# Statistics, normalising, turning and router logits spread from a front stage into the first units of a transformer layer kernel

## The chip, the cores and the metric

The kernel runs on one core of one Trainium2 chip. The metric is the device time of one execution in microseconds (us), the median of several runs. The engines are TensorE (PE), VectorE (DVE), ScalarE (ACT), GpSimd (POOL) and SyncE (SP), which issues nearly all transfers. Each engine works through its own list in order and waits on semaphores for the others.

## The reference

```python
x = L0_attn_x                         # (16, 512, 256), float32
xn = layernorm(x)                     # no scale or shift, eps 1e-5
x = x + attention(xn) + ffn(xn)
# attention: 16 heads of 64, causal, out @ Wo + bo
# ffn: xn + shared_mlp(xn) + sum over the top 2 of 16 experts,
#      chosen by sigmoid(xn @ gate_w + gate_b), weights normalised to 1
# each mlp: (silu(x @ wg) * (x @ wu)) @ wd, hidden size 128
```

## The kernel before

There are B = 16 batches of T = 512 tokens, of width D = 256. A batch in SBUF is 128 partitions by QT = 4 slices by 256 (0.52 MB). Most products run in three passes on a high and a low part of each operand (`HI`, `LO`; `PASSES`), in a rounded 32-bit format; a low part is the value minus its high part.

**Front stage (`stage_a`).** For each batch: load x, `bn_stats` and `bn_aggr` on VectorE (`moments`), a square root on ScalarE, a reciprocal and four normalising operations on VectorE, a store of the normal rows to DRAM (`xn_rows`), eight transposes on TensorE (L280), two copies on ScalarE, and eight matmuls in full float32 for the router's logits (L290, token-major, 16 columns wide). Between these the attention weights, Wo and the shared expert's weights are loaded and split, the high parts on ScalarE and the low parts on GpSimd (L186). A sigmoid over all logits ends the stage; then all engines meet at a barrier.

**Stream (`stream`).** A unit is one pair of heads of one batch: UNITS = 128, eight per batch. `STEPS` goes from -3 to 131; step u works on different units at once: it turns and weighs the probabilities of unit u, makes the scores of u + 1, projects k, v and q for u + 2, and adds the output projection of u - 2. Steps -3 to -1 are the ramp. PSUM is a ring of 8 banks; `order(u)` lists which kinds of work take banks in a step and `emptied` gives the semaphore that frees each. A few times per step SyncE goes through `slot` 0 to 3, paced by TensorE (`pace`), and issues what belongs there.

Batch b's turned rows `xnt[b % 2]` are made in the stream once more, one batch ahead, in units 3, 11, 19, ...: SyncE reloads the normal rows (`load_normal`), TensorE turns them (`turn`, L758), ScalarE copies the high part (L890) and VectorE makes the low part (L1039). GpSimd adds x, the normal rows and bo (`prepare`, L1266 and L1268) in four steps of a batch.

The router's choice (`route`, VectorE, operations of 128x1024) runs in units 0 to 12; rows are scattered to their experts' queues in units 12 to 43 (`FIRST_SCATTER`), the expert tiles (`TICKS`, two per unit) run in units 49 to 89, and their results are gathered and added after that. SyncE clears the queues in DRAM in units 0 to 9 (L521).

Lines that the rows name: L663 projects k or q (six matmuls of 512 columns), L715 weighs v with the probabilities, L878 is ScalarE's copy of a unit's attention output, once per unit, L986 adds the mask and takes the maximum, L860 is the exponential, L1314 GpSimd's division of the probabilities, L979 VectorE's copy of turned probabilities.

## Time and profile before

| | |
|---|---|
| median of 3 runs | 1960.73 us (1960.04 to 1964.51) |
| profiled execution | 1962.58 us, its span 1960.9 us |
| TensorE busy | 1892.3 us (97% of the span) |
| VectorE, ScalarE, GpSimd busy | 72%, 62%, 52% |
| front stage, to the stream's first transfer | 97.2 us |

The span runs from the first to the last instruction. In the stream TensorE is almost always busy, in the front stage and the ramp it is not. The profile's rows give start and length in us; a group's mean is in ns.

### The profile page before, as it was taken

Reading aid. Unit: us, or ns where it says so; the run is one execution under the profiler, and the core shown is the slowest. Engines: PE = TensorE matmul, PEld = TensorE weight load, DVE = VectorE, ACT = ScalarE, POOL = GpSimd, SP = SyncE. Lnnn points to the kernel's source line nnn. Section 1 sums busy time; section 2 is a strip of 40 time slices with the busy share of each in tenths; the row PEclk is TensorE's granted clock in tenths of the full one; section 3 lists DMA queues with packets and bytes.
Section 4 is the critical chain, followed back from the end, with each engine's and each line's share of the span. In section 5 each row is a group of like instructions: output and inputs, shape, how many; then the busy total and the mean of one; then the engine's idle time right before and its main releaser. Section 6 shows DMA issues by size and latency. Waiting matters only on the chain.

```text
span 1960.9 us, 53515 instructions
## 1 busy us (share of the span) xinstructions
PE 1892.3 (97%) x20556; PEld 1748.2 (89%) x20558; DVE 1406.0 (72%) x4086; ACT 1218.2 (62%) x3340; POOL 1020.2 (52%) x1512
## 2 busy tenths in 40 slices
PE   5879999999999999999999999999999999999998
PEld 5868898888889898999999999999999999888897
DVE  7658886767676676666766667667667888878875
ACT  3355566666666565666665666666666666656564
POOL 2133447777776644344343343344344867687742
PEclk9999999999999999999999999999999999999999
DMA  8534422434343312544545445545432232333200
GB/s 246 192 109 175 153 94 82 138 106 146 109 146 109 114 68 71 194 153 148 175 157 178 147 154 167 171 162 173 147 103 77 87 119 87 114 95 120 70 29 12
DMA packets 158603, 249.92 MB, mean 127 GB/s; under 512 B 27280, under 2 KB 112528, under 8 KB 158352
## 3 DMA queue, kind: packets, MB, share of 16 engines
...
q14 instruction: 84, 0.69, 0.1%
...
## 4 chain that ended last, share of the span: by engine, by line
PE 65%; POOL 16%; issue 8%; DVE 3%; ACT 3%; DMA 0%; POOLq 0%; SPq 0%; DVEq 0%
PE d_bank L663 13%; PE d_bank L715 10%; POOL d_probs L1314 9%; PE d_bank L701 9%; PE d_bank L690 8%; PE d_bank L731 6%; PE d_bank L676 6%; PE d_bank L789 6%; POOL queued_rows L1277 4%; PE d_bank L776 3%; ACT d_probs L860 2%; PE d_bank L747 2%; DVE d_probs L986 1%; POOL d_rows L1305 1%; PE d_bank L799 1%
## 5 line engine op out<-in xcount | busy, mean ns | idle before, releaser
L1314 POOL TENSOR_SCALAR d_probs<-d_probs,d_inverse 128x512 f32<-128x512 f32 (+3 forms) x1024 | 554.7, 556 | 756.6 <-DVE d_inverse L992 755.3
L860 ACT ACTIVATE d_probs<-d_probs,d_bias 128x512 f32<-128x512 f32 (+3 forms) x1024 | 562.4, 553 | 119.4 <-DVE d_bias L986 119.4
L986 DVE CUSTOM_DVE_ANT_0 d_probs<-d_bank,mask 128x512 f32<-128x512 f32 (+3 forms) x1024 | 432.5, 484 | 3.2 <-PE d_bank L701 2.5
L663 PE MATMUL d_bank<-d_xnt,wqk_all 128*128 128x512 f32 x1536 | 414.0, 405 | 1.5 <-DVE d_xnt L1039 1.5
L663 PEld LDWEIGHTS d_bank<-d_xnt,wqk_all 128*128 128x128 f32 x1536 | 274.6, 191 | 54.9 <-DVE d_xnt L1039 1.7
L715 PE MATMUL d_bank<-d_probs_t,d_v 128*64 128x128 f32 x5120 | 308.9, 276 | 0.0
L701 PE MATMUL d_bank<-d_ks,d_qs 64*128 64x512 f32 (+3 forms) x3072 | 290.5, 332 | 8.3 <-issue 6.9
L715 PEld LDWEIGHTS d_bank<-d_probs_t,d_v 128*64 128x64 f32 x5120 | 278.1, 137 | 17.1 <-issue 5.4
L701 PEld LDWEIGHTS d_bank<-d_ks,d_qs 64*128 64x128 f32 x3072 | 251.8, 191 | 24.3 <-issue 7.7
L690 PEld LDWEIGHTS d_bank<-ident_r,d_probs_moved 64*128 64x128 f32 x5120 | 226.1, 136 | 48.5 <-issue 48.2
L690 PE MATMUL d_bank<-ident_r,d_probs_moved 64*128 64x64 f32 x5120 | 244.1, 245 | 22.8 <-POOL d_probs L1314 22.0
L853 ACT ACTIVATE d_probs_t<-d_bank 128x512 f32<-128x512 f32 (+1 forms) x384 | 188.2, 525 | 102.1 <-PE d_bank L690 91.9
L997 DVE TENSOR_TENSOR d_qs<-d_bank,d_qs 128x512 fp32r<-128x512 f32 x128 | 88.5, 691 | 201.6 <-ACT d_qs L866 201.6
L878 ACT ACTIVATE d_out_t<-d_bank 128x512 fp32r<-128x512 f32 x128 | 76.4, 597 | 249.5 <-PE d_bank L715 249.5
L979 DVE COPY d_probs_t<-d_bank 128x512 f32<-128x512 f32 (+1 forms) x384 | 209.1, 591 | 8.4 <-PE d_bank L690 7.9
L731 PEld LDWEIGHTS d_bank<-wo_all,d_out_t 128*128 128x128 f32 x1536 | 201.1, 190 | 12.2 <-issue 1.7
L676 PEld LDWEIGHTS d_bank<-wv_all,d_xnt 128*128 128x128 f32 x1536 | 199.4, 190 | 11.1
L731 PE MATMUL d_bank<-wo_all,d_out_t 128*128 128x256 f32 x1536 | 206.7, 281 | 1.5 <-DVE d_out_t L1008 1.5
L676 PE MATMUL d_bank<-wv_all,d_xnt 128*128 128x256 f32 x1536 | 201.2, 281 | 0.0
L860 ACT ACTIVATION_READ_ACCUMULATOR d_probs<-d_probs,d_bias 128x1 f32 x1024 | 194.8, 190 | 0.0
L1008 DVE TENSOR_TENSOR d_out_t<-d_bank,d_out_t 128x512 fp32r<-128x512 f32 x128 | 88.2, 689 | 111.6 <-ACT d_out_t L878 110.7
L1305 POOL DMA_INDIRECT d_rows<-routed_rows,slot x128 | 132.1, 1032 | 34.6 <-issue 34.6
(122 smaller groups left out, 2292.6 us busy)
## 6 DMA issues: line engine op xcount, KB each, us to landing
queued_rows<-d_zeros SPq DMA_DIRECT2D x79, 256.0 KB, 2.4
d_x<-queued_rows SPq DMA_DIRECT2D x79, 256.0 KB, 3.4
routed_rows<-d_y SPq DMA_DIRECT2D x79, 256.0 KB, 2.3
...
a_x_in<-in_L_attn_x SPq DMA_DIRECT2D x16, 512.0 KB, 7.5
xn_rows<-a_xn SPq DMA_DIRECT2D x16, 512.0 KB, 5.2
d_normal<-xn_rows SPq DMA_DIRECT2D x32, 256.0 KB, 3.7
d_base<-in_L_attn_x SPq DMA_DIRECT2D x32, 256.0 KB, 2.9
```

The lines of the kernel that those rows point to most:

```text
L663: last = pe.matmul(to[:, :], wqk[:, n % PAIRS, "qk".index(kind), wa, k, :], xnt[n // PAIRS % 2][:, xb, k, :], start=first, stop=(k == KD - ...
L676: last = pe.matmul(to[:, t * 2 * P:(t + 1) * 2 * P], xnt[b % 2][:, xa, k, tok * P:(tok + 1) * P], wv[:, wb, k, cols], start=(k == 0 and (x ...
L690: last = pe.transpose(to[r][:, off:off + DK].bitcast(F32R), moved[half(r), i, h, j * P:(j + 1) * P], ident[half(r), half(r)])
L701: last = pe.matmul(to[h][:, at * P:at * P + cols], qs[r][qa][half(h), i * P:(i + 1) * P], ks[r][kb][half(h), 0:cols], start=(n == 0), stop ...
L715: last = pe.matmul(to[half(h), i * P:(i + 1) * P], v[u // 2 % 2][:, j, col:col + DK], probs_t[fill][:, h, at + j, :], start=(j == 0), stop ...
L731: last = pe.matmul(to[:, s * D:(s + 1) * D], out_t[g % 2][oa][:, j, cols], wo[:, wb, g % 4 * GROUP + j, :], start=(j == 0 and n == 0), sto ...
L853: act.activation(probs_t[fill][:, :, :, half(0)], bank(f"t{fill}", u)[:, 0:2 * slots * DK].rearrange("p (h j n) -> p h j n", h=2, n=DK), A ...
L860: act.activation(part, part, ACT.Exp, bias=bias[:, i, h:h + 1], scale=-1.0, accum_out=total[which][:, at % 4:at % 4 + 1]).then_inc(exp_don ...
L979: dve.tensor_copy(probs_t[fill][:, :, :, half(1)], bank(f"t{fill}", u, 1)[:, 0:2 * slots * DK].rearrange("p (h j n) -> p h j n", h=2, n=DK ...
L986: dve.tensor_tensor_reduce(out=probs[:, i, h, 0:cols], in0=bank(f"s{fill}", u, h)[:, at * P:at * P + cols], in1=mask[:, T - cols:T], scale ...
L1305: pool.indirect_dma_start(out=rows[m % 4 // 2][:, m % 2 * 2 + n, :], out_offset=None, in_=dram["routed"][:, :], in_offset=bass.IndirectOff ...
L1314: pool.tensor_scalar(part, part, inverse[which][:, at % 4:at % 4 + 1], 1.0, ALU.mult, ALU.mult).then_inc(norm_done, 1)
```

## The change

The front stage keeps the loads and splits of the weights, the gate's weights among them (now in high and low parts), and the statistics of the first four batches (`KEPT`), which stay in SBUF as `xa`; it normalises batch 0. Low parts are shared between VectorE (`ON_DVE`) and GpSimd (`ON_POOL`), and the scale of q's weights goes into the one copy.

In the stream the other twelve batches' rows are loaded for their statistics alone (`load_ahead`) through three buffers, four batches at the end of each of the steps -3, -2 and -1, with one square root for four batches (`deviation`). `FRONT` gives the places where batch n is taken in, two per step, from (-3, second part) for batch 0 to unit 5 for batch 15: GpSimd normalises its rows one place ahead (`normalise_rows`), SyncE stores them, TensorE turns them (`turn`), ScalarE and VectorE make the high and low parts, and one place later six matmuls of 512 columns and 16 output rows make the logits expert-major (`logits`), which ScalarE copies and TensorE turns back one place later still (`logits_back`). The turned rows go to DRAM in high and low parts (`xnt_split`, 1.05 MB per batch) and are loaded for use one batch ahead (`load_xnt`, units 6, 14, ...); the turns of units 3, 11, ... are gone. The rows of batches 4 to 15 are loaded a second time into `xa` (`load_xa`). The sigmoid runs in unit 6. Routing, clearing, scatter and expert tiles all move by `ROUTE_AT` = 7 units.

```diff
 FLEX_AT = 229344 - 32 * 1024
-FIRST_SCATTER = 12
+ROUTE_AT = 7
+FIRST_SCATTER = ROUTE_AT + 12
+KEPT = 4
+GROUPS = [range(b, b + 4) for b in range(KEPT, B, 4)]
...
+                for n, (src, view, _) in enumerate(loads):
+                    sp.dma_start(view, src).then_inc(stage_loaded[n], DMA)
+                    if n < KEPT:
+                        sp.dma_start(xa[n][:, :, :], x_src[n]).then_inc(x_loaded[n], DMA)
+                for n, name in enumerate(("wg", "wu", "wd")):
+                    src = ins["L0_ffn_shared_" + name]
+                    to = shared_in[:, n * WPART:(n + 1) * WPART]
+                    if n < 2:
+                        to, src = to.rearrange("p (k f) -> p k f", k=KD), src.rearrange("(k p) f -> p k f", p=P)
+                    sp.dma_start(to, src).then_inc(stage_loaded[len(loads)], DMA)
 
             @block.gpsimd
             def _(pool):
...
+                pool.tensor_tensor(gate_w[:, LO, :, :], gate_in[:, :, :], gate_w[:, HI, :, :].bitcast(F32), ALU.subtract
+                                   ).then_inc(gate_split, 1)
+                for n in ON_POOL:
+                    _, view, parts = loads[n]
                     pool.wait_ge(stage_hi, n + 1)
                     pool.tensor_tensor(parts[LO], staged_like(view, parts[HI]), parts[HI].bitcast(F32), ALU.subtract
...
-                    if n < KD:
-                        act.activation(view, view, ACT.Copy, scale=-SCALE).then_inc(scaled, 1)
...
+                act.wait_ge(const_loaded, 2 * DMA)
+                act.activation(gate_w[:, HI, :, :], gate_in[:, :, :], ACT.Copy).then_inc(gate_hi, 1)
+                for n in range(len(loads)):
+                    split(n)
+                act.wait_ge(stage_loaded[len(loads)], 3 * DMA)
...
             @block.vector
...
+                def split(n):
+                    _, view, parts = loads[n]
+                    dve.wait_ge(stage_hi, n + 1)
+                    dve.scalar_tensor_tensor(parts[LO], staged_like(view, parts[HI]), -SCALE if n < KD else 1.0,
+                                             parts[HI].bitcast(F32), ALU.mult, ALU.subtract).then_inc(split_dve, 1)
+
+                for b in range(KEPT):
+                    moments(b)
+                    gather(b)
+                    if b < KD:
+                        split(ON_DVE[b])
+                dve.wait_ge(std_done, 1)
+                dve.reciprocal(rstd[:, 0:KEPT * QT], rstd[:, 0:KEPT * QT]).then_inc(rstd_done, 1)
+                dve.wait_ge(rstd_done, 1)
+                for q in range(QT):
+                    dve.tensor_scalar(xa[0][:, q, :], xa[0][:, q, :], mean_var[:, q, 0:1], rstd[:, q:q + 1],
+                                      ALU.subtract, ALU.mult).then_inc(first_normal, 1)
+                split(ON_DVE[KD])
 
...
+        ahead_x = [base[1][:, :, :].rearrange("p q d -> p (q d)"),
+                   *(nc.alloc_sbuf_tensor_at(f"d_ahead_x{hl}", [P, GROUP * T], F32, offset=out_at + (HALVES + hl) * GROUP * T * 4)[:, :]
+                     for hl in range(HALVES))]
...
+        FRONT = {place: n for n, place in enumerate([(-3, 1)] + [(u, part) for u in range(-2, B // 2 - 2) for part in range(2)] + [(B // 2 - 2, 0)])}
...
+                def load_xa(b):
+                    sp.wait_ge(*xn_kept(b - KEPT))
+                    sp.wait_ge(n_ready, (b - KEPT + 1) * KD)
+                    for part in range(2):
+                        two = slice(part * 2, part * 2 + 2)
...
+
+                def store_turned(b, hl):
+                    sp.wait_ge(n_out, (b + 1) * KD)
+                    for k in range(KD):
+                        sp.dma_start(turned_rows(b, hl, k), turned(b)[:, hl, k, :].bitcast(F32)).then_inc(ax_stored[b % 2], DMA)
+
...
+                def load_xnt(b, hl, k):
+                    if hl == 0 and k == 0:
+                        sp.wait_ge(ax_stored[b % 2], (b + 1) // 2 * KD * HALVES * DMA)
+                        if b == 1:
+                            sp.wait_ge(ax_stored[0], (B // 2 - 1) * KD * HALVES * DMA)
+                            sp.wait_ge(lg_ready, B - 1)
+                        else:
+                            sp.wait_ge(p_ready, 2 * PAIRS * (b - 1))
+                            sp.wait_ge(v_ready, PAIRS * (b - 1))
+                    sp.dma_start(xnt[b % 2][:, hl, k, :].bitcast(F32), turned_rows(b, hl, k)).then_inc(xnt_loaded[b % 2], DMA)
+
+                LATER = {place: KEPT + len(ahead_x) + n for n, place in enumerate(
+                    [(-3, slot) for slot in range(4)] + [(-2, 3)] + [(-1, slot) for slot in range(4)])}
+
+                def load_ahead(b):
+                    n = b - KEPT
+                    if n >= len(ahead_x):
+                        sp.wait_ge(stats_done, n - len(ahead_x) + 1)
+                    sp.dma_start(ahead_x[n % len(ahead_x)].rearrange("p (q d) -> p q d", q=QT), x_src[b]
+                                 ).then_inc(ahead_loaded[n % len(ahead_x)], DMA)
 
                 def clear(n):
+                    if n == 0:
...
 
-                        for n in range(u * 8 + slot * 2, u * 8 + slot * 2 + 2):
+                        n = FRONT.get((u, slot // 2))
+                        if n is not None and n <= B:
+                            if slot % 2 == 0 and n < B:
+                                store_xn(n)
+                            if n >= 2:
...
+                def turn(n):
+                    if n:
+                        pe.wait_ge(x_normal, n * QT)
                     for k in range(KD):
-                        to = take(f"n{k}", u)
+                        to = take(f"n{k}", n)
                         for q in range(QT):
-                            last = pe.transpose(to[:, q * P:(q + 1) * P].bitcast(F32R), normal[:, q, k * P:(k + 1) * P],
+                            last = pe.transpose(to[:, q * P:(q + 1) * P].bitcast(F32R), xa_r[n % KEPT][:, q, k * P:(k + 1) * P],
                                                 ident[:, :])
                         last.then_inc(n_ready, 1)
+
+                def logits(n):
+                    to = take("lg", n)
+                    pe.wait_ge(n_out, (n + 1) * KD)
+                    first = True
+                    for k in range(KD):
+                        for wa, xb in PASSES:
+                            last = pe.matmul(to[0:E, :], gate_w[:, wa, k, :], turned(n)[:, xb, k, :], start=first,
+                                             stop=(k == KD - 1 and (wa, xb) == PASSES[-1]))
+                            first = False
+                    last.then_inc(lg_ready, 1)
+
+                def logits_back(n):
+                    to = take("lb", n)
+                    pe.wait_ge(al_done, n + 1)
+                    for q in range(QT):
+                        last = pe.transpose(to[:, q * P:q * P + E].bitcast(F32R), al[:, q * P:(q + 1) * P], ident[0:E, 0:E])
+                    last.then_inc(lb_ready, 1)
 
                 def count(kind, u):
 
@@ -801,6 +831,13 @@
                     last.then_inc(xt_ready, 1)
...
                     act.wait_ge(hidden_done, u // PAIRS + 1)
@@ -932,6 +984,7 @@
                         exponential(3, 1, u + 1)
                         exponential(1, 0, u + 1)
                         exponential(1, 1, u + 1)
+                    front_part(u, 0)
...
-                        split_normal(u)
+                    front_part(u, 1)
+                    if u < 0:
+                        deviation(u + len(GROUPS))
+                    if u == B // 2 - 2:
+                        act.wait_ge(lg_out, B)
+                        act.activation(gates[:, :, :], gates[:, :, :], ACT.Sigmoid).then_inc(sig_done, 1)
...
+                    last.then_inc(mean_done, 1)
+
+                def deviation(g):
+                    cols = slice(GROUPS[g][0] * QT, (GROUPS[g][-1] + 1) * QT)
+                    dve.wait_ge(std_done, g + 1)
+                    dve.reciprocal(rstd[:, cols], rstd[:, cols]).then_inc(rstd_done, 1)
 
                 steps = [0]
...
+                    if u < 0:
+                        for b in GROUPS[u + len(GROUPS)]:
+                            moments(b)
...
+                def normalise_rows(n):
+                    if n >= KEPT:
+                        pool.wait_ge(xa_loaded[n % KEPT], n // KEPT * 2 * DMA)
+                        pool.wait_ge(rstd_done, (n - KEPT) // 4 + 1)
+                    for q in range(QT):
+                        col = n * QT + q
+                        pool.tensor_scalar(xa[n % KEPT][:, q, :], xa[n % KEPT][:, q, :], keep["mean_var"][:, col, 0:1],
+                                           keep["rstd"][:, col:col + 1], ALU.subtract, ALU.mult).then_inc(x_normal, 1)
+
+                normalise_rows(1)
...
```

## Rows read from the trace of the kernel before

**Rows 1.** The page, part 1: busy time of each engine.

```profile
PE 1892.3 (97%) x20556; PEld 1748.2 (89%) x20558; DVE 1406.0 (72%) x4086; ACT 1218.2 (62%) x3340; POOL 1020.2 (52%) x1512
```

**Rows 2.** Windows: length, busy per engine, PEclk, DMA share, GB/s.

```profile
0.00:10.00 10.00, 0.00 (x0) 0.00 (x0) 3.40 (x15) 3.17 (x4) 1.42 (x9) 1.00 0.65 210
...
0.00:27.00 27.00, 13.32 (x75) 13.17 (x75) 16.80 (x71) 11.76 (x20) 3.78 (x10) 1.00 0.81 228
```

**Rows 3.** Groups by form, first 97 us.

```profile
L186 POOL TENSOR_TENSOR wo_all<-a_staged,wo_all 128x2048 fp32r<-128x2048 f32 x1 | 4.5, 4546 | 4.0 <-ACT wo_all L212 4.0
```

**Rows 4.** Timeline of the front stage: start, length, engine, line.

```profile
0.80 0.43 SPq L145 DMA_DIRECT2D a_x_in<-in_L_attn_x  x1
...
4.81 1.41 DVE L236 BATCH_NORM_STATS2 a_stats<-a_x_in 128x6 f32<-128x256 f32 x4 [4.81 <-DMA a_x_in<-in_L_attn_x]
...
6.25 0.38 DVE L240 BATCH_NORM_AGGREGATE a_mean_var<-a_stats 128x2 f32<-128x6 f32 x4
...
10.26 1.38 DVE L251 TENSOR_SCALAR a_xn<-a_x_in,a_mean_var,a_rstd 128x256 f32<-128x256 f32 x4
...
27.14 3.42 DVE L251 TENSOR_SCALAR a_xn<-a_x_in,a_mean_var,a_rstd 128x256 f32<-128x256 f32 x4
...
27.76 2.34 POOL L186 TENSOR_TENSOR wqk_all<-a_staged,wqk_all 128x1024 fp32r<-128x1024 f32 x1 [2.06 <-ACT wqk_all L212]
```

**Rows 5.** Timeline of the seam and the ramp.

```profile
97.23 0.80 SPq L517 DMA_DIRECT2D d_normal<-xn_rows  x2
...
110.69 1.28 ACT L860 ACT_TABLE_LOAD   x1
...
112.46 0.69 DVE L986 CUSTOM_DVE_ANT_0 d_probs<-d_bank,mask 128x512 f32<-128x512 f32 x1 [1.07 <-PE d_bank L701]
...
116.03 2.27 POOL L1314 TENSOR_SCALAR d_probs<-d_probs,d_inverse 128x512 f32<-128x512 f32 x4 [11.20 <-DVE d_inverse L992]
...
119.36 0.99 DVE L979 COPY d_probs_t<-d_bank 128x512 f32<-128x512 f32 x2
```

**Rows 6.** Timeline, ScalarE: the starts of L878 in chosen units.

```profile
134.09 0.60 ACT L878 ACTIVATE d_out_t<-d_bank 128x512 fp32r<-128x512 f32 x1 [1.58 <-PE d_bank L715]
...
203.92 0.60 ACT L878 ACTIVATE d_out_t<-d_bank 128x512 fp32r<-128x512 f32 x1 [4.03 <-PE d_bank L715]
...
243.36 0.60 ACT L878 ACTIVATE d_out_t<-d_bank 128x512 fp32r<-128x512 f32 x1 [3.03 <-PE d_bank L715]
...
344.71 0.60 ACT L878 ACTIVATE d_out_t<-d_bank 128x512 fp32r<-128x512 f32 x1 [2.57 <-PE d_bank L715]
...
371.80 0.60 ACT L878 ACTIVATE d_out_t<-d_bank 128x512 fp32r<-128x512 f32 x1 [2.57 <-PE d_bank L715]
...
384.30 0.60 ACT L878 ACTIVATE d_out_t<-d_bank 128x512 fp32r<-128x512 f32 x1 [1.59 <-PE d_bank L715]
...
409.55 0.60 ACT L878 ACTIVATE d_out_t<-d_bank 128x512 fp32r<-128x512 f32 x1 [3.10 <-PE d_bank L715]
...
1870.87 0.60 ACT L878 ACTIVATE d_out_t<-d_bank 128x512 fp32r<-128x512 f32 x1 [2.58 <-PE d_bank L715]
...
1885.40 0.60 ACT L878 ACTIVATE d_out_t<-d_bank 128x512 fp32r<-128x512 f32 x1 [0.99 <-PE d_bank L715]
...
1897.18 0.60 ACT L878 ACTIVATE d_out_t<-d_bank 128x512 fp32r<-128x512 f32 x1 [2.38 <-PE d_bank L715]
...
1908.96 0.60 ACT L878 ACTIVATE d_out_t<-d_bank 128x512 fp32r<-128x512 f32 x1 [2.85 <-PE d_bank L715]
```

**Rows 7.** Transfers issued in the first 100 us; last: KB, us to landing.

```profile
a_x_in<-in_L_attn_x SPq DMA_DIRECT2D x16, 512.0 KB, 7.5
...
d_normal<-xn_rows SPq DMA_DIRECT2D x2, 256.0 KB, 3.0
```

**Rows 8.** Groups by form on GpSimd, 400 to 420 us.

```profile
L1314 POOL TENSOR_SCALAR d_probs<-d_probs,d_inverse 128x256 f32<-128x256 f32 x4 | 1.9, 478 | 0.0
...
L1266 POOL TENSOR_TENSOR d_base<-d_base,d_normal 128x256 f32<-128x256 f32 x1 | 0.7, 749 | 0.0
```

352 lines of the change are left out of this document (175 added, 177 removed).

## Prediction

> **What bounds the kernel now.** I read the page's busy times first: TensorE is busy 97% of the span and no other engine over 72% [rows 1]. So in the long stream a microsecond taken from or given to TensorE counts whole, and one on VectorE, ScalarE or GpSimd counts only where TensorE ends up waiting. Next the timeline at the seam of the two stages: SyncE issues the stream's first transfer at 97.23 us, the first probabilities are copied at 119.36 us, and unit 0's attention output is ready at 134.09 us, where TensorE has taken over as the bound [rows 5, 6]. The change works in these first 134 us and in the first units. Last, the starts of L878, which runs once per unit, right after TensorE finishes a unit's weighing; their distances are the units' lengths [rows 6].
>
> I call the barrier between stages t0. Before, unit 0 is done at t0+36.9 (134.09 less 97.23) and the first copy of probabilities comes at t0+22.1.
>
> **The front stage.** It loses sixteen batches of turning, fp32 logits, normalising and storing; what is left is bound by loads. It loads six weight halves of 0.52 MB, Wo with 1.05, four batches of 0.52 and 0.39 of shared weights: 6.7 MB. In the first 27 us the trace moves 228 GB/s at a share of 0.81, so 281 GB/s when the engines are full; 6.7 MB take 23.8 us. The first load lands 4.0 us after its issue at 0.80, some 2.4 us more than its own transfer, so the last lands near 27 us [rows 2, 4]. Behind it on GpSimd: ScalarE's high part of Wo ends at about 28.0, GpSimd's low part takes 4.55 [rows 3], to 32.5, and the shared low part about 1.9 more, to 34.4. On VectorE: the square roots come after ScalarE's last copy and a table load, about 30.5, then the first batch's normalising and one low part (the nearest row is four slices of normalising in 1.38 [rows 4]; for 128x1024 I take 1.2, an estimate from that rate). Alone this would end at 33.3. But four such slices took 3.42 instead of 1.38 while GpSimd ran a low part [rows 4], so I let VectorE get through only when GpSimd's Wo is done, at 32.5: 35.7, and 36 with the barrier. Bounds: 34.7 if nothing collides, 43 if loads run at 210 GB/s, the rate of the first 10 us [rows 2]. The term: 36.0 - 97.2 = **-61.2**.
>
> The Trainium skill ("SBUF — State Buffer", section SBUF: two separate sides) says that VectorE and GpSimd share a port pair which one takes for a whole instruction. By that rule, the trace agrees with it here, 3.42 against 1.38; it would lock the two engines against each other in the stage's last 6 us, and not in the later units, where VectorE reads PSUM with one SBUF operand. Without it the stage would be 1.3 us shorter.
>
> **The ramp (steps -3 to -1).** Twelve batches' statistics now stand in VectorE's order, four at the end of each step, each 1.41 + 0.38 = 1.8 us [rows 4]. VectorE, in order, counted from t0:
> Loads 4 to 6 are issued at once, the first lands after 4.0 [rows 4]. Batch 7 waits for a free buffer (about 5.5), then lands by 10. Four moments end at 12.0.
> Step -2 can't end before batch 2 is turned. Its rows are normalised by GpSimd, behind `prepare(0, 0)`, and that waits for the reload of batch 0's normal rows, which SyncE issues only behind `load_ahead(10)`, at 12.5. With 8.7 us of transfers queued in that stretch (8, 9, 10, two stores, this load) it lands near 18. Then two operations of 0.75, four slices of 0.48 [rows 8]: 21.4. Turning (1.3), copies and differences: 24.5. This is the wait that takes the place of the front stage's: VectorE's moments of 8 to 11 and `load_ahead(11)` are queued behind it.
> Moments 8 to 11: 24.5 to 32.1.
> Step -1: root and reciprocal 0.6; a table switch back to the exponential, 1.28 [rows 5]; the maxima, exponentials and normalising for unit 0. Before, GpSimd had done its first four at 118.3, 5.8 us after the first maximum's start at 112.46 [rows 5]. So 39.8; `prepare` 1.5; rows of batch 4, 1.9; turning 1.3; copies and differences 1.9: 46.4.
> Moments 12 to 15 last 7.2 if the data are there. `load_ahead(14)` stands on SyncE behind the store of batch 4 (43.2), and `load_ahead(15)` waits for batch 12's statistics, at 47.8 and then some 5 to 5.5 of landing with stores ahead of it, so the last moments end near 54.9; root and reciprocal: 55.5. Only now does VectorE copy unit 0's probabilities, 33.4 later after t0 than before. From that copy to unit 0's output were 14.7 [rows 5, 6]; one more table switch adds 1.3, the front's work on TensorE is run ahead meanwhile. Unit 0 is done at t0+71.5: **+34.6**. Bounds: +24, if each load lands as fast as the 3.0 of a lone reload, no collision, and GpSimd is never late; +48, if each of the four loads named lands after the 7.5 that loads took in the busy front stage [rows 7].
> The Trainium skill ("ScalarE: Activation LUTs", section What ACT_TABLE_LOAD costs) gives 2.66 us for a switch, with a drain, where the row has 1.28 [rows 5] and shows no drain; the five switches of the ramp and unit 6 would cost 7 us more if all lay on the path. I go by the row.
>
> **Units 1 to 5** each take in two batches. TensorE per batch: eight turns, 0.72 (unit 19, with them, 12.50; unit 123, without, 11.78); six logits matmuls of 512 columns, 0.229 each (unit 121 with twelve such takes 14.53, unit 122 11.78): 1.37; four narrow turns back, at the price of a turn, 0.36. That is 2.45, or 4.9 a unit [rows 6]. The steady units of the same kinds, 17 to 21, took 64.84; less one turn, plus 24.5: 88.6. Before, units 1 to 5 took 203.92 - 134.09 = 69.83 [rows 6]. The term: **+18.8**. It holds as long as TensorE stays the bound. VectorE adds 3.2 a unit and ScalarE 3.6, less than TensorE; GpSimd adds eight slices, 3.8 [rows 8], in gaps where it waits for VectorE's inverses.
> **Unit 6**: four narrow turns and, on ScalarE, the sigmoid with two table loads, 0 to 3.6 on the path. I take 2.0: **+2.4**.
>
> **Routing moved by seven units.** It runs VectorE's long steps of 128x1024. Before, units 1 to 8 took 109.27, units 9 to 16, of the same kinds, 101.35 [rows 6]: 7.9 too much, of which 5.0 in units 1 to 5 are gone from the term above already and 2.9 in units 6 to 8. I let the 7.9 come back in units 7 to 15, where the 2.9 leave: **+5.0** (bounds -3 and 8). Scatter, expert tiles and gathers move as they are and end at unit 125 of 128, still under TensorE: 0.
>
> **Turns taken out of the later stream**: fourteen (units 11, 19, ... 115) at 0.72 [rows 6]: **-10.1**. In their place are transfers: per batch 1 MB stored and 1 MB loaded, the loads a whole batch ahead, hidden in the steady units. For batch 1 alone the load waits for the last store, with about 11 us of TensorE's work to cover 5 to 7: 0, else up to 4.
>
> The sum: -61.2 + 34.6 + 18.8 + 2.4 + 5.0 - 10.1 = -10.5. The profiled execution took 1962.58; 1952.1. The median of the runs is 1.85 below it: **1950.2, told as 1951**.
>
> **The rivals.**
> *The ramp is starved.* Each of the four loads that VectorE waits for lands 3 us later, as in the front stage (7.5 [rows 7]): +13, so 1964. For it: about 15 MB move in 55 us of ramp, 270 GB/s. Against it: the rate of 281.
> *Transfers set the pace of units 0 to 5.* Each unit loads, stores and stores turned two batches: 4.2 MB, with base and normal rows 4.3. In my 17.4 us that is 247 GB/s; TensorE would wait for rows to turn. At 210 GB/s [rows 2] a unit takes 20.5, and six of them +18: 1969, slower than before. It decides from 1.8 us per unit on (224 GB/s), where the gain is gone. Against it: these are 1 to 2 KB runs at 281 GB/s or better.
> *The ramp and routing cost less.* The moments overlap, and moved routing finds slack in its new place: -5 and -8: 1938.
> *The front stage doesn't shrink as far*: within the bounds of 34.7 and 43 above, at worst +7; it is a part of the range, not a case.
>
> **How the numbers follow.** Forecast 0.48, starved ramp 0.20, transfers 0.16, cheap ramp 0.16. The forecast's own range is 1942 to 1960. The likeliest gives 1951; cutting 0.1 at each end of the cases gives 1932 to 1974. A measurement of this kernel tells about 0.3% (5.9 us) from no change, so "faster" is under 1954.9. The forecast case lies there with 0.37 of its 0.48 (0.10 same, 0.01 slower), the cheap ramp whole; the starved ramp is 0.02 faster, 0.10 same, 0.08 slower; transfers 0.03 same, 0.13 slower. Faster 0.55, same 0.23, slower 0.22.
>
> **What the profile after should show.** The stream's first transfer at 35 to 38 us, with GpSimd or VectorE last. The moments in three blocks, VectorE waiting for loads in the first and last, and for GpSimd's rows in the second. The first copy of probabilities at 91, unit 0's L878 at 107.5. L878 spaced by 16.5 to 19.5 in units 1 to 5. Unit 11 and its likes 0.7 shorter. I am wrong if units 1 to 5 are over 19 each, if TensorE waits there for GpSimd's rows, if unit 0 comes before t0+60 or after t0+85, or if narrow logits matmuls cost other than 0.23.

## The result and the profile after

The changed kernel is slower, by 0.7%: 1973.75 us median (1971.92 to 1974.03, 4 runs), the kernel before beside it 1960.38 (1957.36 to 1964.51, 4 runs), a ratio of 1.007, 95% interval 1.005 to 1.009. Its profiled execution took 1973.66 us, the span 1971.9.

The page, part 1, answers [rows 1]. TensorE does 22.6 us less work and the span is 11 us longer, so it stands idle longer:

```profile
PE 1869.7 (95%) x20334; PEld 1704.5 (86%) x20334; DVE 1381.9 (70%) x4017; ACT 1209.2 (61%) x3314; POOL 1089.1 (55%) x1570
```

**The end of the front stage**, timeline. The stage ends at 38.26 where it ended at 97.23 [rows 5]:

```profile
27.77 1.91 ACT L168 ACTIVATE wo_all<-a_staged 128x2048 fp32r<-128x2048 f32 x1 [2.02 <-DMA a_staged<-in_L_attn_Wo]
...
29.76 4.50 POOL L157 TENSOR_TENSOR wo_all<-a_staged,wo_all 128x2048 fp32r<-128x2048 f32 x1 [3.93 <-ACT wo_all L168]
...
32.35 4.50 DVE L211 TENSOR_SCALAR xa<-xa,mean_var,rstd 128x256 f32<-128x256 f32 x4
34.21 1.85 POOL L160 TENSOR_TENSOR shared_all<-a_shared_in,shared_all 128x768 fp32r<-128x768 f32 x1
36.77 1.21 DVE L199 SCALAR_TENSOR_TENSOR wv_all<-a_staged,wv_all 128x1024 fp32r<-128x1024 f32 x1
38.26 0.37 SPq L503 DMA_DIRECT2D d_base<-in_L_attn_x  x1
```

ScalarE waits for Wo until 27.8, where the forecast had the last load near 27. Behind it VectorE's four slices of normalising take 4.50 us where they take 1.38 alone [rows 4]. They start beside GpSimd's low part of Wo and get through only as GpSimd's operations finish: the first slice takes 2.05 us and ends 0.15 behind the low part of Wo, the second 1.89 and ends 0.15 behind the shared one, the other two 0.40 each; GpSimd's two take 4.50 and 1.85, no more than in the kernel before (4.5 [rows 3], and 1.85 in its L189). The Trainium skill ("SBUF — State Buffer", section SBUF: two separate sides) calls the port pair of VectorE and GpSimd an exclusive lock and no split of bandwidth; these rows agree.

**The ramp and the first units.** Timeline of chosen lines:

```profile
57.81 0.72 POOL L1358 TENSOR_TENSOR d_base<-d_base,d_normal 128x256 f32<-128x256 f32 x1 [13.49 <-DMA d_normal<-xn_rows]
...
59.32 9.66 POOL L1415 TENSOR_SCALAR xa<-xa,mean_var,rstd 128x256 f32<-128x256 f32 x8
...
64.21 1.25 PE L770 MATMUL d_bank<-ident_r,d_xa_r 128*128 128x128 f32 x8 [7.75 <-POOL xa L1415]
...
66.83 1.40 DVE L1116 BATCH_NORM_STATS2 stats<-d_ahead_x 128x6 f32<-128x256 f32 x4
...
75.06 1.08 DVE L1116 BATCH_NORM_STATS2 stats<-d_ahead_x 128x6 f32<-128x256 f32 x3 [3.00 <-DMA d_ahead_x<-in_L_attn_x]
...
97.20 1.40 DVE L1116 BATCH_NORM_STATS2 stats<-d_ahead_x 128x6 f32<-128x256 f32 x4 [1.25 <-DMA d_ahead_x<-in_L_attn_x]
...
101.55 1.41 DVE L1116 BATCH_NORM_STATS2 stats<-d_ahead_x 128x6 f32<-128x256 f32 x4 [2.54 <-DMA d_ahead_x<-in_L_attn_x]
...
103.92 1.55 DVE L1036 COPY d_probs_t<-d_bank 128x512 f32<-128x512 f32 x3
```

The eight slices of two batches' rows, 2 and 3, take 9.66 us on GpSimd, 1.2 each and not 0.48. TensorE waits 7.75 for the first four of them, VectorE's next statistics (66.83) stand behind the turning, and the first copy of probabilities (103.92) behind three blocks of statistics. Groups by form on GpSimd, 38 to 130 us, of the changed kernel:

```profile
L1415 POOL TENSOR_SCALAR xa<-xa,mean_var,rstd 128x256 f32<-128x256 f32 x28 | 33.9, 1220 | 2.3 <-POOLq L123 2.3
...
L1406 POOL TENSOR_SCALAR d_probs<-d_probs,d_inverse 128x256 f32<-128x256 f32 x6 | 2.8, 483 | 0.0
```

Both rows are `tensor_scalar` with two steps on the same shape. L1406, as L1314 before it [rows 8], multiplies by one operand per partition and by the constant 1; L1415 takes two operands per partition, subtracts the mean and multiplies by the inverse of the deviation, and costs 2.5 times as much.

**The units.** ScalarE's copy of a unit's output is L913 now and answers to L878 [rows 6]: units 0, 5, 16, 120, 121, 122, 123 and the last.

```profile
121.04 0.60 ACT L913 ACTIVATE d_out_t<-d_bank 128x512 fp32r<-128x512 f32 x1 [1.61 <-PE d_bank L728]
...
207.43 0.60 ACT L913 ACTIVATE d_out_t<-d_bank 128x512 fp32r<-128x512 f32 x1 [1.76 <-PE d_bank L728]
...
353.05 0.60 ACT L913 ACTIVATE d_out_t<-d_bank 128x512 fp32r<-128x512 f32 x1 [2.43 <-PE d_bank L728]
...
1873.85 0.60 ACT L913 ACTIVATE d_out_t<-d_bank 128x512 fp32r<-128x512 f32 x1 [3.05 <-PE d_bank L728]
1891.16 0.60 ACT L913 ACTIVATE d_out_t<-d_bank 128x512 fp32r<-128x512 f32 x1 [0.99 <-PE d_bank L728]
1904.31 0.60 ACT L913 ACTIVATE d_out_t<-d_bank 128x512 fp32r<-128x512 f32 x1 [2.34 <-PE d_bank L728]
1918.74 0.60 ACT L913 ACTIVATE d_out_t<-d_bank 128x512 fp32r<-128x512 f32 x1 [3.17 <-PE d_bank L728]
...
1962.77 0.60 ACT L913 ACTIVATE d_out_t<-d_bank 128x512 fp32r<-128x512 f32 x1 [5.91 <-PE d_bank L728]
```

Against [rows 6]: unit 0 comes 13.1 us earlier, unit 5 is 3.5 late, unit 16 8.3, unit 120 only 3.0, the last one 10.6 (1962.77 against 1952.15 before). The forecast had unit 0 26.6 us earlier. So there are three places of loss: up to unit 0; in the units from 17 to 120, which give back 5.4 and not 9.4; and behind unit 120, where nothing was put down.

Windows of the changed kernel: the ramp with unit 0, the units from 1 on, and unit 121 (length, busy per engine, PEclk, DMA share, GB/s):

```profile
38.26:121.04 82.78, 52.52 (x316) 37.90 (x316) 44.17 (x164) 29.60 (x69) 43.99 (x55) 0.71 0.66 222
121.00:220.00 99.00, 99.00 (x1038) 83.65 (x1038) 62.63 (x184) 65.08 (x168) 70.12 (x88) 1.00 0.70 231
...
1873.85:1891.16 17.31, 16.43 (x156) 14.49 (x156) 12.86 (x34) 8.96 (x24) 14.44 (x21) 0.90 0.37 108
```

In units 1 to 5 TensorE is busy all the time: transfers don't set their pace. In unit 121 GpSimd is busy 14.44 of 17.31 us and VectorE 12.86; before, in the same unit (14.53 us long), they were busy 9.46 and 10.68, and TensorE all the time at a granted clock of 1.00. Now TensorE stands idle for 0.9 us and the clock is 0.90 over the unit: 0.50, the level of 1.2 GHz, from 1877 to 1879, partly so in the microsecond on either side, and 1.00 elsewhere. Lines of the timeline there:

```profile
1872.76 2.51 POOL L1406 TENSOR_SCALAR d_probs<-d_probs,d_inverse 128x384 f32<-128x384 f32 x4
...
1874.95 0.98 DVE L1276 SCALAR_TENSOR_TENSOR d_acc<-d_rows,weight,d_acc 128x256 f32<-128x256 f32 x2
1875.41 0.84 PE L703 MATMUL d_bank<-ident_r,d_probs_moved 64*128 64x64 f32 x16 [0.50 <-POOL d_probs L1406]
1875.43 1.09 POOL L1397 DMA_INDIRECT d_rows<-routed_rows,slot  x1 [0.16 <-issue]
...
1875.86 0.68 DVE L1065 TENSOR_TENSOR d_out_t<-d_bank,d_out_t 128x512 fp32r<-128x512 f32 x1
1876.63 3.55 PE L714 MATMUL d_bank<-d_ks,d_qs 64*128 64x512 f32 x24 [0.38 <-issue]
...
1882.05 1.00 POOL L1397 DMA_INDIRECT d_rows<-routed_rows,slot  x1 [0.31 <-issue]
...
1883.09 2.29 POOL L1406 TENSOR_SCALAR d_probs<-d_probs,d_inverse 128x512 f32<-128x512 f32 x4
...
1891.05 1.18 PE L703 MATMUL d_bank<-ident_r,d_probs_moved 64*128 64x64 f32 x24
```

GpSimd issues six gathers of 1.0 to 1.1 us, one every 1.3 us, between two groups of divisions. The group behind them ends at 1885.4 and TensorE turns its output at 1891.05 without a wait: that one isn't late. TensorE's two waits come earlier. The first, 0.50, is for the group ahead of the gathers, which takes 2.51 us where the next such group takes 1.85: VectorE adds gathered slices beside it (L1276). Its inverses were ready at 1871.6, and GpSimd, which came out of the six gathers of the unit before only at 1869.0 and had other divisions and two additions ahead of it, got to it at 1872.8. The second, 0.38, has no releaser in the profile, but ends 0.09 us after VectorE's L1065, which stands behind the same additions and gives back the bank of unit 120's output. TensorE's waits of 1.07 at 1893.98 and of 0.38 at 1906.91 end 0.10 us after L1065 too. With the slow clock, the scores of L714 then take 3.5 us to the next line where they took 2.05 in this unit before. From 1871 to 1925 there are 20 gathers, before there were 4, and for each a slice is added to the sums (22 of 0.58 us, before 4).

### The profile page after: what moved, and what is told of

Same layout as the page of the kernel before. It is cut to its first block, busy times and chain, and to the rows that moved or that the text cites. A ratio compares the mean times of both kernels' runs of the same rounds, so it can differ in the third digit from the quotient of the medians.

```text
span 1971.9 us, 53180 instructions
## 1 busy us (share of the span) xinstructions
PE 1869.7 (95%) x20334; PEld 1704.5 (86%) x20334; DVE 1381.9 (70%) x4017; ACT 1209.2 (61%) x3314; POOL 1089.1 (55%) x1570
## 4 chain that ended last, share of the span: by engine, by line
PE 64%; POOL 16%; issue 8%; DVE 4%; ACT 3%; DMA 2%; SPq 0%; POOLq 0%; DVEq 0%
PE d_bank L676 12%; PE d_bank L728 10%; POOL d_probs L1406 9%; PE d_bank L714 8%; PE d_bank L703 8%; PE d_bank L744 6%; PE d_bank L689 6%; PE d_bank L819 6%; POOL queued_rows L1369 4%; PE d_bank L806 3%; ACT d_probs L895 2%; PE d_bank L760 2%; DVE d_probs L1043 1%; POOL d_rows L1397 1%; PE d_bank L829 1%
## 5 line engine op out<-in xcount | busy, mean ns | idle before, releaser
L1406 POOL TENSOR_SCALAR d_probs<-d_probs,d_inverse 128x512 f32<-128x512 f32 (+3 forms) x1024 | 560.2, 561 | 739.1 <-DVE d_inverse L1049 737.9
L714 PE MATMUL d_bank<-d_ks,d_qs 64*128 64x512 f32 (+3 forms) x3072 | 293.5, 333 | 16.8 <-ACT d_probs_t L888 9.8
L714 PEld LDWEIGHTS d_bank<-d_ks,d_qs 64*128 64x128 f32 x3072 | 254.8, 192 | 32.3 <-ACT d_probs_t L888 10.5
L913 ACT ACTIVATE d_out_t<-d_bank 128x512 fp32r<-128x512 f32 x128 | 76.6, 599 | 255.3 <-PE d_bank L728 255.3
L1054 DVE TENSOR_TENSOR d_qs<-d_bank,d_qs 128x512 fp32r<-128x512 f32 x128 | 88.6, 692 | 199.4 <-ACT d_qs L901 198.1
L744 PEld LDWEIGHTS d_bank<-wo_all,d_out_t 128*128 128x128 f32 x1536 | 202.7, 189 | 12.7 <-issue 1.7
L1065 DVE TENSOR_TENSOR d_out_t<-d_bank,d_out_t 128x512 fp32r<-128x512 f32 x128 | 88.3, 690 | 119.5 <-ACT d_out_t L913 118.4
```

The source lines that it names most:

```text
L714: last = pe.matmul(to[h][:, at * P:at * P + cols], qs[r][qa][half(h), i * P:(i + 1) * P], ks[r][kb][half(h), 0:cols], start=(n == 0), stop ...
L744: last = pe.matmul(to[:, s * D:(s + 1) * D], out_t[g % 2][oa][:, j, cols], wo[:, wb, g % 4 * GROUP + j, :], start=(j == 0 and n == 0), sto ...
L1406: pool.tensor_scalar(part, part, inverse[which][:, at % 4:at % 4 + 1], 1.0, ALU.mult, ALU.mult).then_inc(norm_done, 1)
```

## The experiments

### The tail: expert tiles seven units later, alone

`tiles_late` is the kernel before with one edit, `before_again` the kernel before once more, in a single run.

```diff
-FIRST_TICK = FIRST_SCATTER + 2 * B + 5
+FIRST_TICK = FIRST_SCATTER + 2 * B + 5 + 7
```

> The kernel before with the expert tiles, and so the gathers behind them, seven units later, and nothing else: front stage, ramp, turns and routing stay. Theory (gathers cost at the end): results are then gathered and added in units 98 to 125 instead of 91 to 118, three items in units 118 to 121 instead of one, two in units 122 to 125 instead of none, where GpSimd and VectorE have no slack; the last units grow by 7 to 8 us in all and the kernel takes about 1968. Rival (the tail is long for another reason, as the transfers or lower clock of the changed kernel): within 2 us of the kernel before, 1959 to 1963.

> The kernel before, unchanged, for its trace on the chip that the next kernels run on. In the two traces so far the changed kernel's steady units are about 0.1 us longer than the same units of the kernel before (for instance 11.96 against 11.87), which eats the 0.7 us per batch that the removed turns should give back. If this is the chip, the units here are as long as in the changed kernel (11.95 or so for a plain unit of the steady stretch). If it is the changed kernel (its transfers of turned rows, or where its tiles lie), they stay at 11.87.

`tiles_late`: 1963.26 (10 runs), before 1959.88 (21 runs), ratio 1.0021 (1.0011 to 1.0030). Its copies of units 120 to 123, timeline:

```profile
1865.88 0.60 ACT L878 ACTIVATE d_out_t<-d_bank 128x512 fp32r<-128x512 f32 x1 [2.96 <-PE d_bank L715]
1883.13 0.60 ACT L878 ACTIVATE d_out_t<-d_bank 128x512 fp32r<-128x512 f32 x1 [0.99 <-PE d_bank L715]
1896.19 0.60 ACT L878 ACTIVATE d_out_t<-d_bank 128x512 fp32r<-128x512 f32 x1 [2.26 <-PE d_bank L715]
1910.70 0.60 ACT L878 ACTIVATE d_out_t<-d_bank 128x512 fp32r<-128x512 f32 x1 [3.16 <-PE d_bank L715]
```

The lengths are 17.25, 13.06 and 14.51, those of the changed kernel (17.31, 13.15, 14.43) and not 14.53, 11.78, 11.78 [rows 6]. From unit 120 to the last this kernel takes 87.1 us, `before_again` 81.4 (1872.4 to 1953.8). So moving the tiles lengthens the last units by itself, by 5.7, where 7 to 8 were expected. The median grew by only 3.4, under the expected 1968, and the traces show one reason: units 17 to 120, which the tiles leave and enter, take 1523.1 us against 1526.2 in the first trace of the kernel before and 1530.6 in `before_again`. The move gains something there.

`before_again` took 1964.21, with plain units of 11.86 to 11.87 as in the first profile, so the 0.1 us of the changed kernel's units isn't the chip's. The two traces of the unchanged kernel differ by 2.3 us in the front stage (97.2, 94.9), 1.2 in the ramp with unit 0 and 4.5 in units 17 to 120; terms taken from one trace each are known no better than that.

### The ramp: what GpSimd's rows cost

`one_pointer` is the changed kernel with GpSimd multiplying by the inverse deviation alone and an immediate in place of the second operand; the mean is left out of the rows of batches 1 to 15.

```diff
-pool.tensor_scalar(xa[n % KEPT][:, q, :], xa[n % KEPT][:, q, :], keep["mean_var"][:, col, 0:1],
-                   keep["rstd"][:, col:col + 1], ALU.subtract, ALU.mult).then_inc(x_normal, 1)
+pool.tensor_scalar(xa[n % KEPT][:, q, :], xa[n % KEPT][:, q, :], keep["rstd"][:, col:col + 1], 1.0,
+                   ALU.mult, ALU.mult).then_inc(x_normal, 1)
```

> The changed kernel, but GpSimd's normalising in the stream multiplies by the deviation's inverse and the constant 1 and no longer subtracts the mean (so the output leaves the mean out for batches 1 to 15): one operand per partition read from SBUF in place of two. Theory: the second such operand is what makes a slice of 128x256 take 1.23 us where the division of probabilities of the same size takes 0.48; a slice takes about 0.48, each batch's rows come 3 us sooner, and unit 0 is ready 7 to 9 us sooner after the front stage, so about 1965. Rival (GpSimd is slowed by VectorE beside it, or by the operand's place): slices stay near 1.2 us, and the time near 1974. A third: slices get short but SyncE's queue and the loads then hold VectorE, so under 4 us are won.

1965.17 (1963.35 to 1967.39, 10 runs), before 1959.88, ratio 1.0032 (1.0022 to 1.0042), 8.6 us under the changed kernel. Groups by form, as above:

```profile
L1415 POOL TENSOR_SCALAR xa<-xa,rstd 128x256 f32<-128x256 f32 x33 | 15.2, 485 | 2.3 <-POOLq L123 2.3
```

485 ns, the price of the divisions: the operand of the mean costs the other 0.74 us. The edit takes away two things together, the second operand per partition and the subtraction; no run has one without the other. Unit 0 comes at 114.7, 6.3 earlier, where 7 to 9 were expected.

### The ramp: statistics later

`late_moments` takes the statistics of batches 8 to 15 out of steps -2 and -1 and does them in steps -1, 0 and 1; their loads and roots move with them (left out of the cut).

```diff
+MOMENTS_AT = {-3: range(4, 8), -1: range(8, 11), 0: range(11, 14), 1: range(14, 16)}
...
-for b in GROUPS[u + len(GROUPS)]:
+for b in MOMENTS_AT.get(u, ()):
```

> The changed kernel with the statistics spread wider: batches 4 to 7 in step -3 as now, 8 to 10 in step -1, 11 to 13 in unit 0, 14 and 15 in unit 1, with the roots behind units 0 and 1. Theory: VectorE's blocks of statistics and their loads stand on the chain to unit 0 in steps -2 and -1 (from about 67 to 77 and from 92 to 103.4 us in the trace), while in units 0 and 1 TensorE is the bound and VectorE has room; unit 0 comes 12 to 18 us sooner, units 0 and 1 grow by up to 4, so 1960 to 1965. Rival: the chain is held by GpSimd's rows anyway, and unit 0 comes at most 5 us sooner (1969 or more).

1966.64 (6 runs), ratio 1.0041 (1.0028 to 1.0054). The copies of units 0 and 1:

```profile
105.29 0.58 ACT L915 ACTIVATE d_out_t<-d_bank 128x512 fp32r<-128x512 f32 x1
...
132.60 0.57 ACT L915 ACTIVATE d_out_t<-d_bank 128x512 fp32r<-128x512 f32 x1
```

Unit 0 is 15.7 us earlier, but the next unit takes 27.3 where it took 18.2, and at unit 16 only 4.4 are left. Most of the block's cost moved with it, and the time is above the 1960 to 1965 expected.

### Wo's low part, and the first batches' rows, on VectorE

`wo_on_dve` exchanges Wo for a weight half among the low parts and puts VectorE's last one ahead of its wait for the root:

```diff
-ON_DVE, ON_POOL = (0, 1, 5), (2, 3, 4, 6)
+ON_DVE, ON_POOL = (0, 1, 6), (2, 3, 4, 5)
...
+split(ON_DVE[KD])
 dve.wait_ge(std_done, 1)
...
-split(ON_DVE[KD])
```

> The changed kernel with the low part of Wo made by VectorE and that of v's second half by GpSimd, in the front stage alone. Theory: GpSimd's Wo (29.8 to 34.3 us) and VectorE's first batch that stood blocked behind it (4.50 instead of 1.38) set the end of the stage; now it ends at 34.5 to 36 instead of 38.3, and the whole is 2 to 4 us shorter, 1970 to 1972. Rival: loads or the root set the end, and the stage still ends at 38.

1970.01 (5 runs), before 1959.30 (24 runs), ratio 1.0050 (1.0034 to 1.0066): 3.7 under the changed kernel, as expected. The front stage ends at 35.1, unit 0 comes at 118.1.

`rows_and_wo_on_dve` adds that VectorE normalises batches 1 to 4, in the order in which it is free for them; GpSimd starts with batch 5.

```diff
+                normalise_rows(1)
                 for u in STEPS:
...
+                    if u == -1:
+                        normalise_rows(4)
                     front_part(u, 0)
...
+                    if u == -3:
+                        normalise_rows(2)
+                        normalise_rows(3)
...
-                    if n is not None and n + 1 < B:
+                    if n is not None and FIRST_ON_POOL <= n + 1 < B:
```

> The changed kernel with the rows of batches 1 to 4 normalised by VectorE (1 to 3 at the start of the stream, while it waits for loads, 4 in step -1; GpSimd does 5 to 15), and Wo's low part on VectorE as in the run beside it. Theory: GpSimd's 4.85 us per batch and its place behind the reload of normal rows leave the chain to unit 0: from the front stage's end to unit 0 in 65 to 71 us instead of 82.7, the front stage 3 shorter, 1957 to 1963 in all. Rival: loads hold VectorE's statistics, and only the 3 us that GpSimd's second batch cost are won: 1967 to 1970.

1955.67 (1952.21 to 1958.44, 10 runs), before 1959.30, ratio 0.9985 (0.9973 to 0.9997), less than the 1957 to 1963 expected. Timeline: VectorE's eight slices for batches 2 and 3, and the copy of unit 0:

```profile
37.77 2.66 DVE L1135 TENSOR_SCALAR xa<-xa,mean_var,rstd 128x256 f32<-128x256 f32 x8
```

```profile
104.99 0.60 ACT L914 ACTIVATE d_out_t<-d_bank 128x512 fp32r<-128x512 f32 x1 [1.44 <-PE d_bank L729]
```

VectorE takes 2.66 for what took GpSimd 9.66, both with two operands per partition. Unit 0 is at 105.0, that is t0+69.9, where the forecast had t0+71.5 for a ramp with cheap rows in another order; in `wo_on_dve`, without the move of the rows, it was t0+82.9. Units 1 to 5 are unchanged (18.25, 16.85, 16.85, 17.54, 16.92).

`rows_wo_spread` is this kernel with eight of the statistics in pairs in steps -1 to 2.

> As the run beside it, and the statistics spread two batches a step: 4 to 7 in step -3, then 8 and 9 in step -1, two each in units 0, 1 and 2, roots behind units 0 and 2. Theory: nothing but the first four batches' statistics is left ahead of unit 0, which comes 45 to 52 us after the front stage; units 0 to 2 pay 4 to 8 us of it back, since VectorE's lists there grow by 3.6 us each; 1945 to 1953, faster than both kernels. Rival: what unit 0 wins, units 0 and 1 give back wholly, as three quarters of it were in the run with late statistics, and the time is that of the run beside it.

1958.40 (10 runs), ratio 0.9992 (0.9980 to 1.0004). Unit 0 comes at 93.0, 12 us earlier, the next units take 20.9, 25.3 and 20.6, and unit 5 comes at 194.3, later than the 191.4 without it. The expected 1945 to 1953 was missed and the rival held: a pair of statistics in a unit, with its loads and roots, costs more there than in the ramp.

### The steady units: where the stream's tiles lie

A plain steady unit is 0.1 us longer in the changed kernel (units 33 to 34), in which the stream's tiles begin at byte 92800 of a partition and not at 92096, because 708 bytes were taken ahead of them to hold logits. `shifted_tiles` is the kernel before with an unused tile of that size there.

```diff
+sb("spare", [P, 177])                 # ahead of the stream's tiles
```

> The kernel before with an unused tile of 708 bytes per partition placed where the changed kernel has one, so that every tile of the stream lies 704 or 708 bytes further on, and nothing else. Repeated traces have a plain steady unit at 11.87 us in the kernel before and at 11.97 in the changed kernel and each variant of it. Theory (where the tiles lie): the units here are 11.97 too, and the kernel takes 8 to 11 us longer, 1968 to 1971. Rival (the transfers of turned rows, the semaphores waited for, or the order of PSUM banks): units stay at 11.87 and the time at 1960.

1966.42 (8 runs), before 1959.30, ratio 1.0031 (1.0018 to 1.0044). Copies of units 33 and 34 in the kernel before and in `shifted_tiles`:

```profile
563.65 0.60 ACT L878 ACTIVATE d_out_t<-d_bank 128x512 fp32r<-128x512 f32 x1 [0.99 <-PE d_bank L715]
575.51 0.60 ACT L878 ACTIVATE d_out_t<-d_bank 128x512 fp32r<-128x512 f32 x1 [2.57 <-PE d_bank L715]
```

```profile
563.40 0.60 ACT L878 ACTIVATE d_out_t<-d_bank 128x512 fp32r<-128x512 f32 x1 [0.99 <-PE d_bank L715]
575.37 0.60 ACT L878 ACTIVATE d_out_t<-d_bank 128x512 fp32r<-128x512 f32 x1 [2.67 <-PE d_bank L715]
```

11.86 and 11.97, and the changed kernel has 11.97 (571.91 to 583.88): an unused tile alone makes a plain steady unit 0.1 us longer. The time grew by 7.1, a little under the 8 to 11 expected. TensorE doesn't wait in either unit; its own matmuls take longer. From the projection of k to the start of the weighing, in the same two kernels:

```profile
567.34 1.65 PE L663 MATMUL d_bank<-d_xnt,wqk_all 128*128 128x512 f32 x6
...
573.06 2.40 PE L715 MATMUL d_bank<-d_probs_t,d_v 128*64 128x128 f32 x40
```

```profile
567.10 1.66 PE L663 MATMUL d_bank<-d_xnt,wqk_all 128*128 128x512 f32 x6
...
572.91 2.40 PE L715 MATMUL d_bank<-d_probs_t,d_v 128*64 128x128 f32 x40
```

5.72 against 5.81 us, 0.03 more in each of three kinds of matmul: the projections of k and q together, that of v, and the output projection. The weighing takes 2.33 from its start to the next line in both.

I then tried 772 bytes in place of 708, which puts the tiles at the same remainder by 256 as in the kernel before: in the kernel before, in the changed kernel, and in `rows_and_wo_on_dve`.

> The kernel before with the same unused tile of 772 bytes, so that its stream's tiles start at byte 92864. Theory: units at 11.86 to 11.87 and no change in time (1958 to 1961), where the tile of 708 bytes made them 11.97 and cost 7 us. Rival: 11.97 and 1965 or more.

> The changed kernel with its unused tile 64 bytes per partition longer: the stream's tiles start at byte 92864 instead of 92800; in the kernel before it is 92096. 92864 and 92096 leave the same rest by 128 and by 256, 92800 another. Theory (the start counts by its rest): plain steady units are back at 11.86 to 11.87, and the kernel takes 5 to 9 us less than the changed one, 1965 to 1969. Rival (where a tile lies counts in larger steps, or the distance to the tiles in front): units stay at 11.97 and the time at 1974.

> The version with the rows of batches 1 to 4 and Wo's low part on VectorE, and the tile 64 bytes longer. If the three causes add up (GpSimd's rows 14, the front stage 3, the tiles' place 7): 1947 to 1951, faster than the kernel before by 0.5%. If the place counts for nothing here: 1955.

1967.77 (5 runs), 1972.88 (5) and 1955.47 (11), before 1960.11 (20 runs); ratios 1.0036, 1.0066 and 0.9982, each as without the 64 bytes, units of 11.96 to 11.98. The theory, a rule of the remainder by 256 alone, fell. Four single runs of the kernel before with other shifts (64, 256, 512 and 832 bytes):

> The kernel before with an unused tile of 68 bytes, so that the stream's tiles start 64 bytes further on (92160 instead of 92096). A step at any other start: a plain steady unit takes 11.97 instead of 11.87. If only a long way counts: 11.87.

> The kernel before with the stream's tiles 256 bytes further on. If the start counts by its rest by 128 or 256: a plain steady unit at 11.87. If another start always costs: 11.97.

> The kernel before with the stream's tiles 512 bytes further on. If the start counts by its rest by 512: a plain steady unit at 11.87. If another start always costs: 11.97.

> The kernel before with the stream's tiles 832 bytes further on, the longest way that there is room for. If there is a threshold between 512 and 704 bytes: 11.97. If some starts are good and others not without such order: either.

| tiles begin at | plain units (33 to 34; 46 to 47) | time |
|---|---|---|
| 92096 (before) | 11.86; 11.78 | 1960.38 (1 run beside these) |
| +64, +832 | 12.01, 12.02; 11.93 | 1971.86, 1970.18 (1 run each) |
| +256, +512, +768 | 11.98, 11.97, 11.98; 11.89 | 1964.46, 1964.62 (1 run each), 1967.77 (5 runs) |
| +704 | 11.97; 11.91 | 1966.42 (8 runs) |

Starts with one remainder by 256 (64 and 832; 256, 512 and 768) do give one length, but the unshifted start has the remainder of the second row and is still the fastest. In these runs the distance to the tiles at fixed addresses changes as well, so either could be what counts; that stays open.

`after_tiles_back` puts the tiles of the changed kernel back at 92096. The logits' rows go, in two halves of 1 KB, where routing's tiles come later, ScalarE copies them in two steps, and one small tile of routing moves out of the way.

```diff
-sb("spare", [P, 177])
...
-keep["al_rows"] = nc.alloc_sbuf_tensor_at("al_rows", [E, T], F32, offset=al_at)
+al_at = [nc.sbuf_base - 4 * TT * 4 - SLOT_TILES * 4, FLEX_AT + 119 * 256]
+keep["al_rows"] = [nc.alloc_sbuf_tensor_at(f"al_rows{n}", [E, T // 2], F32, offset=at) for n, at in enumerate(al_at)]
```

> The changed kernel with the stream's tiles back at the address that they have in the kernel before (92096; the changed kernel has them at 92800). The 2 KB of the logits' rows, which needed the room in front of them, are split into two halves of 1 KB kept where routing's own tiles come later, so ScalarE copies them in two steps of 256 columns. Theory of placement: the plain steady unit falls from 11.97 back to 11.87, which over units 17 to 119 gives back 8 to 10 us, and a little more in the last units: 1962 to 1965 where the changed kernel has 1973.75. Rival: the 0.1 us of the changed kernel comes from its own work (rows turned loaded from DRAM in the steady units) and only looks like that of the placement: units stay at 11.97 and the time at 1972 to 1975. Second rival, from the looks in which every shift of the kernel before, 64 to 832 bytes, made units slower: it is the distance to the tiles of fixed address that counts; it gives the same as the theory here, as both come back together.

1964.68 (1960.39 to 1967.36, 12 runs), before 1960.40 (17 runs), ratio 1.0023 (1.0014 to 1.0032): 9.1 us under the changed kernel. Units 33 and 34:

```profile
570.79 0.60 ACT L914 ACTIVATE d_out_t<-d_bank 128x512 fp32r<-128x512 f32 x1 [0.99 <-PE d_bank L728]
582.66 0.60 ACT L914 ACTIVATE d_out_t<-d_bank 128x512 fp32r<-128x512 f32 x1 [1.84 <-PE d_bank L728]
```

11.87 again. The 0.1 us was the placement's and not that of the transfers which replaced the turns. It isn't in every unit: against the changed kernel, 54 of the 104 units from 17 to 120 are 0.04 to 0.2 us shorter, 4.9 us in all. The other 3.0 of the 7.9 us between the two traces come in jumps of single units, up to 2 us and both ways, such as also differ between the two traces of the unchanged kernel. The 9.1 in the medians is the firmer number.

### The best version

`last_four_late` is `rows_wo_64_on` with the statistics of batches 12 to 15 alone moved, two each to units 0 and 1. `last_four_tiles_back` is the same with the tiles back at 92096.

> As the run beside it, and only the last four batches' statistics moved, two behind unit 0 and two behind unit 1, with their rows (12 to 14) loaded ahead in step -1 so that VectorE needn't wait for them. Theory: the two earlier spreads gave their gain back because VectorE waited in units 0 and 1 for loads (1.6 us once) and because everything of three steps met there; with the loads ahead, 3 to 6 of the 7.4 us block in step -1 stay won: 1943 to 1947. Rival: VectorE's and ScalarE's lists in units 0 and 1 are full in any case (the root's two table loads, two batches taken in), and the time is that of the run beside it or 2 us more.

> The best version so far (rows of batches 1 to 4 normalised on VectorE, Wo's low part on VectorE, the last four batches' statistics in units 0 and 1; 1955.28) with the same tiles back at 92096. Theory of placement: the two gains add, 1944 to 1947, a ratio of 0.992 to 0.994 to the kernel before. Rival: the gain of placement was bought by the waits of the ramp or the tail and doesn't come: 1953 to 1957.

`last_four_late`: 1955.28 (1951.74 to 1957.34, 9 runs), ratio 0.9975 (0.9966 to 0.9985), which its parent's interval (0.9972 to 0.9992) overlaps; the expected 1943 to 1947 was missed and the rival held: unit 0 comes at 97.9 and not 105.1, unit 5 at 189.9 and not 191.5. `last_four_tiles_back`: 1948.20 (1943.80 to 1951.39, 6 runs), before 1960.40, ratio 0.9934 (0.9918 to 0.9949), the fastest of all and just above the 1944 to 1947 expected. Its profiled execution was the slowest of the six. The copies of units 0 and 5:

```profile
97.14 0.60 ACT L917 ACTIVATE d_out_t<-d_bank 128x512 fp32r<-128x512 f32 x1 [2.63 <-PE d_bank L731]
...
191.07 0.60 ACT L917 ACTIVATE d_out_t<-d_bank 128x512 fp32r<-128x512 f32 x1 [1.71 <-PE d_bank L731]
```

## Why the prediction was wrong

The sum was -10.5 to the profiled execution's span; the spans differ by +11.0. Term by term, from the first trace of each kernel:

| term | forecast | measured | off by |
|---|---|---|---|
| front stage | -61.2 | -59.0 | +2.2 |
| ramp and unit 0 | +34.6 | +45.9 | +11.3 |
| units 1 to 5 | +18.8 | +16.6 | -2.2 |
| units 6 to 16: 2.4 and 5.0, less one turn | +6.7 | +4.8 | -1.9 |
| units 17 to 120: 13 turns | -9.4 | -5.4 | +4.0 |
| from unit 120 to the end | 0 | +8.0 | +8.0 |

**The ramp, the largest error, failed first at one price: "four slices of 0.48 [rows 8]".** The row was the right shape and engine, but with one operand per partition. The edit's operation has two, 1.22 us a slice, 4.9 for a batch and not 1.9. `one_pointer` takes 6.3 us off unit 0, so this price explains 6.3 of the 11.3. The chain itself was read rightly, in its own order: `prepare` waits for the reload and starts at t0+19.5 (forecast 18), the rows of batch 2 end at t0+25.9 (21.4), and the statistics of batches 8 to 11 start at t0+28.6 (24.5).

**The starved ramp, a rival, is true for most of the rest.** The forecast had VectorE wait for loads in the first block of statistics and in the last, and there for 1.3 us. In the first the waits (1.12 and 1.82) fit its sum: the block ends at t0+12.7 (12.0). In the second, where it named none, VectorE waits 3.00 for the load of batch 11, and the block takes 10.1 us and not 7.6. In the third it waits 1.25 and 2.54, and the block takes 10.9 and not 8.5. Together these are 4.9 us, from the rows; no run has the loads alone earlier. `rows_and_wo_on_dve`, which takes these rows off GpSimd and from behind `prepare`, has a ramp of 69.9, 12.9 shorter: that is price and order together, and doesn't tell them apart.

**"Scatter, expert tiles and gathers move as they are and end at unit 125 of 128, still under TensorE: 0" is the step that failed at the other end.** I asked only whether the moved work ends in time. Moved by seven units it came to units 120 to 127, where TensorE's work leaves no slack: 8.0 in the traces. `tiles_late` shows 5.7 of such a loss with nothing else changed. The rows of unit 121 name what TensorE waited for, divisions that GpSimd reached late and VectorE slowed, and a bank that VectorE gave back behind its additions; that these are the cause is argued from the rows. Where the granted clock fell, TensorE had waited shortly before, but the clock stayed at 1.00 after a wait of 2.18 in the kernel before (1859.97) and of 1.07 here (1893.98), so what makes it fall isn't shown. Nor is the size steady: from unit 120 to the last the changed kernel and its variants take between 83.8 and 89.1 us, and 83.8 in `after_tiles_back`, with the order of work unchanged; why is open. Nor do these rows bear out the forecast's remark that the lock would not reach the later units: L1276 reads two tiles in SBUF, and GpSimd's four divisions of 384 beside it take 2.51 to 2.67 us where they take 1.85 without it.

**The turns came out as priced, and two terms were missing.** In `after_tiles_back` a unit that lost its turns is 0.7 us shorter than in `tiles_late` (unit 67: 16.83 against 17.54), and units 17 to 120 take 1512.9 us (353.1 to 1866.0) against 1523.1: -10.2, for 13 turns priced at 9.4. The first missing term is that the moved tiles themselves shorten this stretch, by 3.1 or 7.6 depending on the trace of the kernel before. The second is placement, 7.9 between the traces and 9.1 between the medians. Nothing in the trace of before shows that price; that the change allocates 708 bytes ahead of the stream's tiles stood in the code and I passed over it. Without it `after_tiles_back` is still slower than before, so the ramp and the tail are enough for the wrong sign. Its trace is of a run 4.1 us under its median, so the terms read from it are on the short side.

**Right:** the front stage within its bounds (38.26, forecast 34.7 to 43), with GpSimd and VectorE last; the lock between them, only that it held VectorE behind the shared low part as well, and not behind Wo's alone; TensorE as the bound of units 1 to 5, which take 86.4 us (88.6 forecast) while 252 GB/s are moved, so that the rival of transfers setting the pace fell; the price of the narrow logits matmuls, six in 1.56 us, as long as six of 512 columns and full width take (L760, 1.56); the wait for GpSimd's rows as the one that takes the front stage's place.
